# Eight PSUM banks dealt out anew in the latent attention: two for scores and five for the ring, in place of three and four

## The reference

```python
x = x + _L0_xattn_ref(_layernorm(x), ctx_4096, Wq_d, W_qk, Wkv_d, Wv_u)  # 16 heads, scores in a latent space of 32
x = x + _L0_ffn_ref(_layernorm(x), weight_q, scale, zero_point, bias)    # 512 x 512, int4 weights
x = x + _L1_xattn_ref(_layernorm(x), ctx_4096, Wq, Wk, Wv, Wo)           # 16 heads of 96, 4 groups of keys, keys: context + x
x = x + _L1_ffn_ref(_layernorm(x), W, b, A, Bmat, LiMEs)                 # 512 x 512 and a mixture of low rank
```

## Time and profile before

| | |
|---|---|
| median of 3 runs | 1916.51 us (1914.15 to 1917.76) |
| the profiled execution's own time | 1919.0 us |
| its span in the trace | 1917.2 us |
| TensorE busy, share of the span | 97% |
| VectorE, ScalarE | 53%, 47% |
| second stage | about 318 to 1,010 us |
| granted clock of TensorE, mean | 0.979 of full |

### The profile page before, as it was taken

The page is one execution under the profiler, slowest core; times in us unless marked ns, Lnnn a source line. Parts: engine busy times, 40 slices in busy tenths (PEclk is TensorE's granted clock), DMA queues, the critical chain, the costliest instruction groups (busy, mean ns, idle before and its releaser), DMA issues.

```text
span 1917.2 us, 23300 instructions
## 1 busy us (share of the span) xinstructions
PE 1854.1 (97%) x8602; PEld 1328.9 (69%) x8602; DVE 1007.4 (53%) x1857; ACT 906.5 (47%) x1727; POOL 686.5 (36%) x646
## 2 busy tenths in 40 slices
PE   7999998999999999999889999999999999999998
PEld 6999996454565465555577777767777677767764
DVE  3455555666555655656535545554455555554415
ACT  2333332454344344434236666645666466655560
POOL 0000000000110100100037777766777577766770
PEclk9999998999999999999899999999999999999998
DMA  5989944000112020021177434444554255444101
GB/s 171 293 266 284 282 168 150 0 1 18 55 34 62 12 78 23 22 80 34 55 218 167 127 114 112 103 118 118 137 126 116 52 134 145 126 118 111 58 26 44
DMA packets 196070, 208.82 MB, mean 109 GB/s; under 512 B 90545, under 2 KB 160689, under 8 KB 195958
## 3 DMA queue, kind: packets, MB, share of 16 engines
q1 hardware_dynamic: 181254, 189.45, 34.7%
q10 hardware_dynamic: 14704, 17.89, 3.0%
HBM read 129.30 MB, written 77.94 MB: 108 GB/s over the span
## 4 chain that ended last, share of the span: by engine, by line
PE 73%; DVE 4%; ACT 2%; POOL 1%; issue 1%; DMA 1%; SPq 0%; ACTq 0%; POOLq 0%; DVEq 0%
PE ps L1101 9%; PE ps L1719 6%; PE ps L1720 6%; PE ps L1742 6%; PE ps L1721 6%; PE ps L1739 6%; PE ps L1740 5%; PE ps L1652 5%; PE ps L1160 5%; PE ps L1086 5%; PE ps L1112 4%; PE ps L1675 3%; PE ps L1196 2%; ACT pr L1223 1%; PE ps L1689 1%
## 5 line engine op out<-in xcount | busy, mean ns | idle before, releaser
L1634 POOL TENSOR_TENSOR pl<-pf,ph 128x512 fp32r<-128x512 f32 (+1 forms) x480 | 623.6, 1320 | 255.5 <-ACT pf L1821 255.3
L1818 ACT ACTIVATE ph<-ps 128x512 fp32r<-128x512 f32 (+1 forms) x480 | 288.4, 601 | 357.7 <-PE ps L1721 357.7
L1901 DVE TENSOR_REDUCE pm<-ps 128x1 f32<-128x464 f32 x480 | 307.2, 641 | 242.6 <-PE ps L1652 239.6
L1329 DVE TENSOR_REDUCE pm<-ps 128x1 f32<-128x400 f32 (+3 forms) x512 | 268.8, 572 | 98.6 <-PE ps L1160 82.6
L1223 ACT ACTIVATE pr<-ps 128x512 f32<-128x512 f32 (+1 forms) x416 | 219.2, 601 | 189.1 <-PE ps L1086 182.5
L1821 ACT ACTIVATE pf<-ps 128x512 f32<-128x512 f32 (+1 forms) x480 | 289.5, 603 | 1.0 <-POOL pl L1634 0.8
L1101 PE MATMUL ps<-pr,cv 128*64 128x512 f32 (+1 forms) x832 | 209.9, 623 | 0.0
L1739 PE MATMUL ps<-ph,vh 128*97 128x512 f32 (+1 forms) x480 | 192.5, 401 | 0.0
L1742 PE MATMUL ps<-pl,vh 128*97 128x512 f32 (+1 forms) x480 | 190.0, 396 | 0.8 <-POOL pl L1634 0.8
L1740 PE MATMUL ps<-ph,vl 128*97 128x512 f32 (+1 forms) x480 | 189.4, 395 | 0.0
L124 POOL TENSOR_TENSOR ast<-turned_row,negid 8x1024 fp32r<-8x1024 f32 x15 | 28.4, 1891 | 422.4 <-DVE turned_row L1340 422.4
(11 more groups left out here) (304 smaller groups left out, 3222.8 us busy)
## 6 DMA issues: line engine op xcount, KB each, us to landing
woT<-wo_turned SPq DMA_DIRECT2D x30, 768.0 KB, 6.1
v_scr<-vst SPq DMA_DIRECT2D x16, 1152.0 KB
cnat<-in_ctx_dram SPq DMA_DIRECT2D x16, 768.0 KB, 8.5
q_scr<-qst SPq DMA_DIRECT2D x48, 256.0 KB, 2.5
vh<-v_scr SPq DMA_DIRECT2D x15, 672.0 KB
vl<-v_scr SPq DMA_DIRECT2D x15, 672.0 KB
k_scr<-home SPq DMA_DIRECT2D x24, 384.0 KB, 7.9
home<-k_scr SPq DMA_DIRECT2D x13, 696.4 KB, 8.5
```

The costliest lines, as they stand in the source:

```text
L1329: dve.reduce_max(pm[:, j, ch:ch + 1], src[:, 0:(cuts if s < S else next_cuts)[ch][1]], AX)\
L1634: pool.tensor_tensor(pl[0:m, n % 2, cols], pf[0:m, half, :], ph[0:m, n % 2, cols].bitcast(F32), ALU.subtract).then_inc(plo, 1)
L1818: act.activation(ph[0:keys[kt], n % 2, cols], src, ACT.Exp, scale=S1).then_inc(phi, 1)
L1901: ins = dve.reduce_max(pm[:, j, ch:ch + 1], at[:, 0:cuts[ch][1]], AX)
```

## The change

Of the eight banks, the score half tiles get banks 0 and 1 (were 0 to 2), the gathered values bank 2 (was 3), and the ring banks 3 to 7 (were 4 to 7).

```diff
@@ latent_attention_and_ffn
     NU = NQ + NKL + TT
-    OB, M0, RB, SB = 3, 4, 4, 3
+    OB, M0, RB, SB = 2, 3, 5, 2
     HW = HD0 + 1
```

## The result

The changed kernel takes 1935.41 us (median of 4 runs, 1931.91 to 1939.78) against 1915.33 us: ratio 1.0114, 95% interval 1.0093 to 1.0134, some 22 us slower by the ratio. It lies in the range that was given, 12 us under the value predicted: +20 to +22 us where +31 was forecast. The direction and the mechanism came out as forecast; what gives time back was put too low.

What follows compares the result with a forecast made beforehand. TensorE, busy 97% of the span, was taken as the bound, its waits in the second stage deciding. Score banks +35, ring -4, clock and rest 0 gave +31 us: 1,947 us; 1,936 to 1,960 at 0.7, 8-in-10 range 1,929 to 1,963.

Steps and rivals of the forecast that it cites:

- Score banks, three to two: Second stage: 66 waits for exponentials each grow 0.50 us, plus 2 us of new waits; +35 us, bounds 27 to 40.
- Ring, four banks to five: Second stage: a fifth bank releases TensorE one maximum earlier in seven places; -4 us, bounds 0 and 14 us gained.
- a bank behind q items gives nothing: Ring waits at steps' starts (line 1378): the score behind would wait for its exponential instead, some 0.2 us.
- rival 2: Half the delay is hidden: ring waits vanish, clock falls partly; 35 - 14 - 5 = +16, 1,925 to 1,935 us; chance 0.13.
- The clock: Second stage's four clock falls, 10 us: taken as 0, range widened 10 us down and 20 to 40 up.
- the first rival: Clock goes down in twelve more second-stage places, 1.7 to 3.4 us each; +20 to +40, 1,967 to 1,987 us; chance 0.1.
- The rest: Values' bank and its copy, DMAs, SP and POOL queues, and product groups from 922 us on: unchanged, 0.
- the third: Fifth ring bank worth more than the third score bank: 35 - 52 = -17, 1,900 us; chance 0.03.

Runs made afterwards that it cites:

- Experiment 6: The change's banks, with each second-stage exponential taking 256 of 512 columns, against the kernel before: ratio 1.0020 (same halving with the banks of before: 0.9969).
- experiment 2: Three score banks and a ring of three, one bank idle, against the kernel before: ratio 1.0110, some 21 us slower.
- experiment 3: Four score banks, one for values and a ring of three, against the kernel before: ratio 1.0070.
- experiment 7: Banks of before, more ring products between a pair's two score tiles (shares 4, 2, 1 for 2, 2, 3), against the kernel before: ratio 1.0011.

## Why the prediction came out as it did

1. *Score banks, three to two: +35 us.* Right, in mechanism and size. A pair grows by 0.50 us, 0.28 with halved exponentials. In the timelines it is 33.3 us in 75 places, 34.3 in 77 without the fifth bank.
2. *Ring, four banks to five: -4 us.* Mis-sized, and put down to the wrong cause. Over all profiles the part with scores is 587.9 - 567.4 = 20.5 us longer in the mean, so 33.3 - 20.5 = 12.8 us came back. The clock's windows account for up to 5.9 of them, which leaves about 7 for ring waits (in the two profiles first compared, 14.1 came back, of which the clock's part is up to 10.3 - 1.7 = 8.6). I had put the ring's part at seven places times one reading, gained by the fifth bank. But the run with two score banks and a ring of four, its clock's part taken off, gives back 34.3 - (587.0 - 559.8) = 7.1 us without a fifth bank, and the bank adds about 1. What gives the time back is that TensorE, held longer at the scores, waits less for the ring. The sum had that at nothing, and rival 2 named it. The split between clock and waits rests on windows of the clock and was not made by an experiment. The claim that a bank behind q items gives nothing held: where the ring wait went (2.1 us to none), the score wait behind it took its place. In four of these six places the distance grew by 0.1 us, in two by 0.35, where 0.2 was forecast.
3. *The clock: 0 us.* Mis-sized: -6 us by the profiles, within the 10 us that the range allowed for. I had set shorter ring waits against longer score waits and called them even. Longer waits of 0.9 us with scores and maxima between them brought no steady new falls; the falls that returned at two places of the kernel before, where ring waits of 0.17 and 0.76 us stand ahead of eight short matmuls, went. What causes the falls is not shown. Experiment 6 has falls at 505 and 669 us behind two ring waits of 0.5 us each before maxima, with none before line 1168, but no fall behind the same two at 831 to 833; and the seven waits of 0.8 to 1.0 us behind q items in experiments 2 and 3 have none. The Trainium skill's "TensorE: Matmul & The Clock Gate", in "A second HAM failure mode: psum-queue depth-cycling", tells of a kernel whose rotation through PSUM banks made the clock swing; from this the first rival took that two score banks would bring more swings. The runs here don't bear that out: 0.983 to 0.987 against 0.979 to 0.987, and fewer falls in the stage.
4. *The rest: 0.* Held, within what one profile differs from the next.
5. A slip of place: the stretches at 490, 656 and 820 us that I called a batch's first step lie behind the feed-forward products at its first step's end, in its second step. The four waits that I placed in the third step of a batch lie mostly in its first (459 to 462, 624 to 626 and 789 to 791 us; one, at 395, is in a third). No number hangs on it.

The sum by the profiles is +33 - 6 - 7 = +20 us, against +31. Rival 2 (35 - 14 - 5 = +16, up to 1,935 us), to which I gave 0.13, is what happened, 12 us under the forecast and inside the range; that the range reached so far down is owed to that rival. The sign in the rivals held as well: the third, that the fifth bank is worth more than the third score bank, needs 35 us and the bank has about 1, or 6 with the clock.

What stays open: why the clock falls where it does, which decides some 6 us of the change and, in experiments 3 and 7, much of what shorter waits seemed not to give. Taking away 20 to 25 us of the weight load's waits gained nothing (experiment 7) or 8 us (experiment 3); TensorE's own loss fell by 13 and 15 us there, and ring waits (2.0 to 9.1 us) and the clock took most of the rest. Of the versions that do all the work, none is faster than the kernel before.

## What to carry to other kernels

When a bank is taken from a rotation, read from the timeline which reader's end the writer would then wait for, and count the places where it waits already: each grows by the pitch of one reading, here 0.50 us, whatever the engines' busy shares say. What the bank gives elsewhere is worth less where two waits stand in line, since the second takes over from the first. And a wait in a trace is not its own price: a weight load's wait is longer than what TensorE loses by it (25 us against 15 in experiment 3), and where another engine is a little behind, waits in one place take from those in the next (33 us added cost 26 here, before the clock). And before a difference of some 6 us is put down to a change, the clock of the parts that it doesn't touch wants a look: here it differed by up to 12 us.

## What was not expected of the hardware

The granted clock rose, from 0.981 to 0.985 in the median of the runs, though TensorE waits more in sum. The falls did not follow the sum of waits; of the 40 falls between 340 us and the last row of maxima in the 14 profiles, 34 come within 3 us or so of a ring wait of 0.5 us or more, while the seven waits of 0.8 to 1.0 us at steps' starts (experiments 2 and 3) brought none. A separate group of values in float32, with its weight load in front, costs TensorE some 0.24 us more than the same four instructions in a longer group.
